# A delta-rule walk whose output is formed transposed, chunk by chunk, in place of padded score matrices

## What is computed

```python
def step(S, inp):                                  # S: (B, 8, 32, 32)
    qt, kt, vt, bt = inp
    Sk = jnp.einsum('bhk,bhkv->bhv', kt, S)
    S = S + jnp.einsum('bh,bhk,bhv->bhkv', bt, kt, vt - Sk)
    ot = jnp.einsum('bhk,bhkv->bhv', qt, S)
    return (S, ot)
_, os_ = jax.lax.scan(step, S0, (qs, ks_, vs, bs))
o = jnp.moveaxis(os_, 0, 1).reshape(Bb, Ll, Dd)
...
return (o - mu) / jnp.sqrt(var + 1e-05) * ln_w + ln_b
```

## Time and profile before

| | us |
|---|---|
| median of 3 runs | 3181.72 |
| lowest, highest | 3176.04, 3186.53 |
| profiled execution | 3179.42 |
| its span | 3177.4 |
| PE busy | 2491.4 (78%) |
| PE weight loads busy | 2195.7 (69%) |
| DVE busy | 1483.2 (47%) |
| ACT busy | 1157.8 (36%) |
| POOL busy | 926.0 (29%) |

### The profile page before, as it was taken

The page is one execution under the profiler, slowest core; times in us unless marked ns, Lnnn a source line. Parts: engine busy times, 40 slices in busy tenths (PEclk is TensorE's granted clock), DMA queues, the critical chain, the costliest instruction groups (busy, mean ns, idle before and its releaser), DMA issues.

```text
span 3177.4 us, 54420 instructions
## 1 busy us (share of the span) xinstructions
PE 2491.4 (78%) x20928; PEld 2195.7 (69%) x20928; DVE 1483.2 (47%) x3604; ACT 1157.8 (36%) x2426; POOL 926.0 (29%) x1216
## 2 busy tenths in 40 slices
PE   4678868888688886888868888678877888777688
PEld 3567757777577775787657776568766777666578
DVE  3434553445534445444454444545444444544541
ACT  2235432445225442245412544134432354323223
POOL 2123323233223232233323223232322233233233
PEclk7679988999799997999979998789987999898799
DMA  6000000000000000000000000000000000000000
GB/s 202 1 1 1 3 12 15 1 1 18 19 7 1 1 18 21 4 1 1 20 21 3 1 8 21 14 1 1 15 14 14 1 1 10 12 15 6 21 10 7
DMA packets 86976, 43.33 MB, mean 14 GB/s; under 512 B 71472, under 2 KB 81584, under 8 KB 86704
## 3 DMA queue, kind: packets, MB, share of 16 engines
q1 hardware_dynamic: 83040, 28.12, 3.5%
q0 software_dynamic: 3664, 11.53, 1.1%
HBM read 27.05 MB, written 12.58 MB: 12 GB/s over the span
## 4 chain that ended last, share of the span: by engine, by line
PE 46%; DVE 25%; ACT 10%; issue 10%; POOL 5%; DMA 3%; SPq 1%; DVEq 0%; POOLq 0%; ACTq 0%
PE F L1218 21%; DVE prod L1079 4%; DVE ti L1081 3%; PE Q L1261 3%; PE F L1240 2%; PE Q L1329 2%; PE Q L1346 2%; PE Q L1308 2%; POOL hA_lo L580 2%; DVE hid L899 2%; PE Q L1444 2%; PE Q L1414 1%; PE Q L1381 1%; PE Q L1300 1%; PE Q L1312 1%
## 5 line engine op out<-in xcount | busy, mean ns | idle before, releaser
L1218 PE MATMUL F<-hA_hi,h_sb 128*128 128x256 f32 x2048 | 568.1, 311 | 107.8 <-POOL hA_lo L580 107.4
L580 POOL TENSOR_TENSOR hA_lo<-hid,hA_hi 128x256 fp32r<-128x256 f32 (+1 forms) x384 | 353.0, 920 | 879.2 <-ACT hA_hi L706 494.0
L1218 PE MATMUL F<-hA_lo,h_sb 128*128 128x256 f32 x2048 | 542.9, 299 | 0.0
L1218 PE MATMUL F<-hB_hi,h_sb 128*128 128x256 f32 x2048 | 526.1, 295 | 0.3
L1218 PEld LDWEIGHTS F<-hA_hi,h_sb 128*128 128x128 f32 x2048 | 426.6, 208 | 127.9 <-POOL hA_lo L580 115.4
L1218 PE MATMUL F<-hB_lo,h_sb 128*128 128x256 f32 x2048 | 508.8, 287 | 0.0
L1198 PE MATMUL F<-xf_hi,w_sb 128*128 128x256 f32 x1024 | 319.0, 338 | 162.6 <-DVEq L902 69.2
L1218 PEld LDWEIGHTS F<-hA_lo,h_sb 128*128 128x128 f32 x2048 | 428.3, 209 | 0.5
L1218 PEld LDWEIGHTS F<-hB_hi,h_sb 128*128 128x128 f32 x2048 | 400.8, 196 | 19.0 <-issue 15.3
L1218 PEld LDWEIGHTS F<-hB_lo,h_sb 128*128 128x128 f32 x2048 | 401.7, 196 | 0.3
L1198 PEld LDWEIGHTS F<-xf_hi,w_sb 128*128 128x128 f32 x1024 | 234.9, 229 | 183.8 <-DVEq L902 82.9
(11 more groups left out here) (212 smaller groups left out, 4492.7 us busy)
## 6 DMA issues: line engine op xcount, KB each, us to landing
h_sb<-h_dram POOLq DMA_DIRECT2D x2, 4096.0 KB, 24.5
x_sb<-x_dram SPq DMA_DIRECT2D x8, 512.0 KB, 3.9
a_scr<-q_sb SPq DMA_DIRECT2D x128, 32.0 KB, 1.7
au<-a_scr SPq DMA_DIRECT2D x8, 512.0 KB, 3.2
t_scr<-ti SPq DMA_DIRECT2D x8, 512.0 KB, 3.0
tbd<-t_scr SPq DMA_DIRECT2D x128, 32.0 KB, 1.9
out_dram<-x_sb SPq DMA_DIRECT2D x8, 512.0 KB, 3.3
w_sb<-w_dram POOLq DMA_DIRECT2D x3, 1024.0 KB, 9.0
```

The source lines that it names most:

```text
L580: pool.tensor_tensor(lo, hid[:, n % 2, 0:w, :], hi.bitcast(F32), ALU.subtract).then_inc(f_lo.handle, 1)
L1218: last = pe.matmul(ps[:, i * TOK:(i + 1) * TOK], w[:, k, o:o + P], part[:, k, :], start=(i == 0 and k == 0 and part is src[0]), stop=(i == ...
```

## The change

The output of a tile is now formed transposed in `Q[2]`: features in partitions, tokens in columns. Four things follow.
- `query` swaps its operands: `sbd` is the weight matrix (128 x 128), 32 columns of `qT` stream, and the result is 128 partitions x 32 columns. For chunk 0 it waits for `d_oT` instead of `d_done`.
- The score products are formed chunk by chunk, straight behind the chunk's `k^T u`: 8 matmuls with weights `u` 32 x 32 and 32 columns of `pc` streaming. POOL's 4 copies a tile and its memset of `pbd` are gone, and so are the 8 matmuls of line 1444.
- Behind the last chunk, ACT copies the transposed output into `oT` (signal `d_oT`). In the ninth step PE waits for that and transposes it back, 2 transposes, into bank `Q[1]`. Before it does, it waits until ACT has copied the next tile's `u` out of `Q[1]` (`d_ur`).
- DVE reads the output from `Q[1]`, so `form_uw` of a tile waits for `d_done` of two tiles before.

```diff
-                pbd = s3_("pbd", [P, DH, P])
+                oT = s3_("oT", [P, G, P])
...
+        def ot_step(t):
+
+            return D20 + D2_STEPS * t + 2 * NB - 1
... (POOL)
-                own(pool.memset(pbd[:], 0.0))
                 pool.sem_inc(d_clear.handle, 1)
                 for t in range(NT):
                     yield D20 + D2_STEPS * t
-                    if t:
-                        pool.wait_ge(d_o.handle, d_o.at(b, t))
-                        pool.sem_inc(pool_gate, 1)
-
-                    own(pool.memset(pool_pad[:], 0.0))
-                    for c in range(NB):
-                        s = slice(BLK * c, BLK * (c + 1))
-                        own(pool.tensor_copy(pbd[s, :, s], pc[s, t]))
-                    pool.sem_inc(d_pbd.handle, 1)
... (ACT)
+                def copy_o(t):
+
+                    act.wait_ge(d_oTp.handle, d_oTp.at(b, t + 1))
+                    act.copy(oT[:].rearrange("p g n -> p (g n)"), Q[2][:, 0:D]).then_inc(d_oT.handle, 1)
+
...
+                    if t:
+                        yield ot_step(t - 1)
+                        copy_o(t - 1)
+                yield ot_step(NT - 1)
+                copy_o(NT - 1)
... (DVE)
-                    own(dve.tensor_scalar(on[:], Q[2][:, 0:D], dmv[:, 0:1], drs[:], ALU.subtract, ALU.mult))
+                    own(dve.tensor_scalar(on[:], Q[1][:, 0:D], dmv[:, 0:1], drs[:], ALU.subtract, ALU.mult))
...
-                    own(dve.bn_stats(dbst[:], Q[2][:, 0:D]))
+                    own(dve.bn_stats(dbst[:], Q[1][:, 0:D]))
... (PE, form_uw)
+                    if t > 1:
+
+                        pe.wait_ge(d_done.handle, d_done.at(b, t - 1))
... (PE, query)
-                        pe.matmul(Q[2][s, g * P:(g + 1) * P], qT[:, t, g, s], sbd[:, g, :],
-                                  start=(g == 0), stop=False, skip_group_check=True)
+                        o = g * P + BLK * c
+                        pe.matmul(Q[2][:, o:o + BLK], sbd[:, g, :], qT[:, t, g, s],
+                                  start=(c == 0 and g == 0), stop=False, skip_group_check=True)
... (PE, the walk)
-                                pe.wait_ge(d_done.handle, d_done.at(b, t))
+                                pe.wait_ge(d_oT.handle, d_oT.at(b, t))
...
                         last.then_inc(d_sp.handle, 1)
+                        for h in range(DH):
+                            r = slice(HD * (h % 4), HD * (h % 4 + 1))
+                            o = h // 4 * P + BLK * c
+                            last = pe.matmul(Q[2][r, o:o + BLK], u_sb[t % 2][s, h, :], pc[s, t, h, :],
+                                             start=False, stop=True, skip_group_check=True)
+                        if c == NB - 1:
+                            last.then_inc(d_oTp.handle, 1)
...
-                    pe.wait_ge(d_pbd.handle, d_pbd.at(b, t + 1))
-                    for h in range(DH):
-                        last = pe.matmul(Q[2][:, h * HD:(h + 1) * HD], pbd[:, h, :], u_sb[t % 2][:, h, :],
-                                         start=False, stop=True, skip_group_check=True)
+                    pe.wait_ge(d_oT.handle, d_oT.at(b, t + 1))
+                    if t + 1 < NT:
+
+                        pe.wait_ge(d_ur.handle, d_ur.at(b, t + 2))
+                    for g in range(G):
+                        last = pe.transpose(Q[1][:, g * P:(g + 1) * P], oT[:, g, :], ident[:])
                     last.then_inc(d_o.handle, 1)
```

More of the change, by code:

```diff
@@ L398, in hybrid_kernel @@
         d_tbd = Signal(sem("d_tbd"), NT * NB * 16)
-        d_pbd = Signal(sem("d_pbd"), NT)
+        d_oTp = Signal(sem("d_oTp"), NT)
+        d_oT = Signal(sem("d_oT"), NT)
         d_uwp = Signal(sem("d_uwp"), NT)
```

## The result

| | before | changed |
|---|---|---|
| median, us (19 runs each, same chips) | 3182.77 | 3191.73 |
| lowest, highest | 3176.04, 3186.94 | 3180.90, 3212.48 |
| ratio, 95% interval | | 1.0034 (1.0021 to 1.0046) |
| span of the profiled execution | 3177.4 | 3182.2 |
| PE busy | 2491.4 | 2484.6 |

The change makes the kernel 0.34% slower. That lies inside the predicted range (3165 to 3199), but the forecast was no change, and this is just past the 0.3% that the prediction called the limit of what can be told. The profiled execution took 3184.12 us, so it is one of the quicker ones: it is 4.7 us over the profiled execution of before, where the medians are 9.0 apart, and its trace can explain only half of the loss. The first thing to see is the spread: 10.9 us between the extremes before, 31.6 after.

What follows compares the result with a forecast made beforehand. Neither PE (78% busy) nor DVE alone sets the time, though the first walk is close to PE-bound. Walks -6.0 plus clock +7.2 gave +1 us on 3179.4; with the median 2.3 higher, it said 3182, range 3165 to 3199.

Steps and rivals of the forecast that it cites:

- The walk at full clock: PE's shift through a walk's four tiles: +0.96, -1.06, -1.10, -0.60 us; -6.0 us over all walks.
- Scores: 128 chunks, 8 small matmuls behind `k^T u`: 0.14 us a group, bounds 0.14 and 0.26.
- Queries: 128 query products with full weight loads, not beside `w S`: +0.22 us, bounds 0 and 0.45; free where PE waits for `u`.
- Output step: End of tile: 1.80 us of matmuls become copy and transposes; +0.24 us in tile 0, -1.50 tile 1, -0.90 tile 2.
- Waits: Chunk 0 stops waiting for `normed_o`: 1.08 us gained in tile 1, nothing in tile 3; new waits and POOL savings nothing.
- The clock: Half clock behind PE idles, including the new 1.6 us at tile 0's end: five falls in eight at 1.44 us, +7.2.
- Half clock in tile 1 in all eight walks: Sign listed under what would show the prediction wrong, at the start of tile 1.
- the list of chances: Forecast's own case 0.58, holding sums from about -9 to +9; none to eight clock falls put at -7 to +4.
- rival B: PE waits for ACT's copy behind the GELU; falls there in all walks, tile 3 in half: +11, 3193 us; chance 0.14.

Runs made afterwards that it cites:

- warm3: Changed kernel plus 12 useless PE matmuls in each of three long idles a walk (end of tile 0, chunk 1 of tiles 2 and 3): 3158.36 us, 0.9947.
- warmbefore: Kernel before the change plus 12 useless matmuls ahead of `w S` of chunk 1 of tile 2: 3178.68 us, 1.0006.
- donewait: Changed kernel with the old wait put back, chunk 0's query product again waiting for `normed_o` of the tile before: 3211.83 us, 1.0107.
- after_again: Changed kernel run again unaltered, for a second profile: 3204.35 us, 1.0072 against the kernel before.
- normlater: Changed kernel with `normed_o` of the tile before moved behind the masking of chunk 0 in DVE's list: 3171.13 us, 0.9975.
- splitact: normsplit with the copy of tile 0's output back on ACT, behind the GELU slice: 3153.59 us, 0.9930.
- normsplit: normdve with `normed_o` cut in two, first part behind the masking of chunk 0, the rest behind that of chunk 1: 3126.74 us, 0.9843.
- warm0: Changed kernel plus 12 useless matmuls at the end of tile 0, ahead of the wait for the copied output: 3183.24 us, 1.0009.
- noscore: Changed kernel without the score products, but for one small matmul a tile that carries the signal: 3188.80 us, 1.0027.
- normdve: normlater with DVE instead of ACT copying the transposed output of tile 0: 3152.84 us, 0.9908.

## Why the prediction was right and where it was wrong

**The walk at full clock: right, with 0.5 us missed.** warm3 and warmbefore show both kernels without a fall. From the first `w S`, the later tiles start at 17.17, 33.31 and 52.76 us in warm3 and at 16.24, 34.50 and 54.24 in warmbefore: +0.93, -1.19, -1.48 for +0.96, -1.06, -1.10 predicted. At the last `w S` it is -1.28 (63.73 against 65.01), for -0.82 predicted (the -0.60 of the sum has the last query behind it). The piece missed is tile 2: the statistics with which its chain through DVE begins start 1.2 us earlier (33.41 against 34.61) and chunk 1 starts 1.40 earlier (38.67 against 40.07), where I had 1.0 for both.

**Scores: right.** In chunk 2 of tile 0, with no wait around, the changed kernel has (L1394 transposes `u`):

```profile
500.72 0.33 PE L1438 MATMUL Q<-u_sb,kn 32*32 32x32 f32 x16
500.87 0.31 PE L1445 MATMUL Q<-pc,u_sb 32*32 32x32 f32 x16
501.11 0.44 PE L1394 MATMUL Q<-ident,uT 128*128 128x128 f32 x2
```

The scores start 0.15 us behind `k^T u`, and the next kind of matmul comes 0.39 us behind it, where it was 0.26 before: a group added 0.13. Taken: 0.14, the lower bound. The page "TensorEngine Tiling (Array Packing)" of the Trainium skill, section Instruction Overhead, gives each matmul an overhead of about 60 cycles. The prediction added these up one behind the other, to an estimated 0.40 us a group; the trace speaks against adding them up here, with 0.13.

**Queries: right.** `w S` to the FFN takes 0.81 us where the query has no wait to hide in (501.60 to 502.41 in the changed kernel), 0.57 before; +0.24 for +0.22.

**Output step: right.** Tile 0 at 2.09 us, tile 2 at 0.98, tile 1 covered; predicted 2.09, 0.96, covered. (The 0.12 us for the signals in that sum came from no row; the 0.98 bears the sum out, not each term.)

**Waits: right.** Chunk 0 in tile 3 lost its wait and chunk 1 waits 1.34 us, 0.9 longer than before for "about 1.1". donewait prices tile 1's at 1.1 for 1.08.

**The clock: the step that failed.** "I take five falls in eight: +7.2". There were three errors in it. It took five falls, each at the price of the old one (3.4 us at half), where all eight walks fell and seven of them stood at half for 6.8 us. It had the old fall at tile 2 stay, and that went in all eight walks of the first profile. And it took the price from two distances inside the walk (1.44 us) as a price in the program's time; warmbefore took the six falls of the kernel before away and gained nothing. "Half clock in tile 1 in all eight walks" is the sign that the prediction itself named for being wrong, and it came. Inside the walks the clock costs 9 us in the kernel before (529.4 against 8 x 65.0) and 24 in the changed one (533.5 against 8 x 63.7): +14 to +15 in place of +7.2. The same figures give the change -10 at full clock in place of -6, so the two errors partly cancel in the profiled execution: -10 and +14 to +15 leave the +4.1 us that the walks show, for +1 predicted. That the time still fell inside the range is in part luck. (In the list of chances, the sum with no fall is -6 and with eight +5.5, not -7 and +4.)

The executions near the median were not profiled. What the two profiles suggest for them is rival B: falls at tile 3 as well, in two walks of the execution of 3184 us and in five of that of 3206. B gave 3193 with a chance of 0.14. Its places were right; that its time came out too is luck, since it had each fall at 1.44 us, where some last 13.7 us (after_again), and the walk at full clock at -6 in place of -10.

The sign: at full clock the change would be faster. warm3 has its whole work and more and is 0.53% faster than the kernel before. Against warmbefore, the old kernel filled in the same way, it is 20 us faster, 12.4 of them inside the walks (510.2 us in all against 522.6).

What stays open is what decides whether the clock falls behind a given wait, and for how long: behind waits of the same length it stayed at half for 3.4, 6.8 or 13.7 us, or did not fall. The traces show one thing that goes with it. Ahead of nearly every walk the clock stands at half for over 20 us, and where that ends against the first `w S` differs. Walk 1 and walk 3 of the kernel before (their first `w S` at 492.28 and 1261.84):

```profile
464.40:491.70 27.30, 14.20 (x83) 0.50 0.11 29
...
1235.80:1259.60 23.80, 11.28 (x69) 0.50 0.09 28
1259.80:1261.80 2.00, 2.00 (x18) 1.00 0.34 53
```

Walk 1 had full clock again 0.5 us ahead and fell at tile 2; walk 3 had it 2.1 us ahead and did not. The walks that kept their clock behind the 1.6 us at the end of tile 0 (walks 4 and 5 of donewait, 5 and 6 of normlater, 8 of splitact) had it 2.1 to 2.2 us ahead too. In the two profiles of the changed kernel, walk 7 aside, the five walks that had it 0.43 to 0.57 us ahead fell in tile 3 and the nine that had it 0.60 to 0.93 ahead did not. So with the same waits, a difference of less than 2 us in where they lie against that earlier change of the clock goes with a fall or none. No run moved this alone, so it is not shown to be the cause. The distances between walks gather at some 376, 382, 385.6, 389 and 392.7 us over the runs, with some in between; what sets that was not tested either.

## What to carry to other kernels

An idle of PE is priced by what it does to the clock behind it as well as by its length: here a wait of 1.6 us in place of 0.8, at a place where the old kernel worked, cost 27 us over eight walks (splitact against normsplit), and only some 6 of them are the longer wait. Whether a given idle brings a fall could not be told from its length; filling all such idles with useless matmuls for one run tells what they cost (warm3); filling one of them can just move the fall (warm0). When a change replaces matmuls with a wait for another engine, look at what stands ahead of that engine's step in its own list (here a GELU slice), and put the copy where that engine is free or put queued matmuls ahead of the wait. And when a change frees a dependency, look for the order that it allows: the gain was in moving the normalization, which no part of the change had used.

## What the runs showed of the hardware that I had not expected

- Half clock under full load. In after_again PE was busy 13.37 of 13.40 us (551.5 to 564.9) and the clock stayed at 0.50 throughout; the usual stretch was 3.4 or 6.8 us.
- The same waits, no fall: donewait's walks 4 and 5 kept the full clock behind waits of 1.62, 1.41 and 1.58 us.
- Less work, no faster: noscore has fewer matmuls than the changed kernel, and six of its eight walks took 66.6 us or more, where most of the changed kernel's took 66.3 in the first profile. More work, faster: warm3, 36 useless matmuls a walk, 0.53% under the kernel before, where the changed kernel is 0.34% over it.
- The spread of a kernel's runs hints at this. The changed kernel's 19 runs span 32 us; the three kernels with no fall inside a walk (normdve, normsplit, warm3) span 6 to 9, though with only 4 to 6 runs each. It is no proof of a steady clock: warm0, with falls in every walk, spans 8 us in 12 runs.
- A saving need not arrive. In warmbefore 1.4 us a walk were gained, and two thirds of it were lost again within 17 us of the walk's end, through a longer half-clock stretch.
